# Attention of a two-part transformer block: heads one by one from three bf16 parts, and two heads on row halves from two fp16 parts

## What is computed

```python
    h = _layernorm(x, axis=-1) * (1 + ca) + sa
    x = x + ga * _L0_attn_ref(h, ...)
    h = _layernorm(x, axis=-1) * (1 + cb) + sb
    x = x + gb * _L0_ffn_ref(h, ...)
...
        Q, K, V = proj(Wq, bq), proj(Wk, bk), proj(Wv, bv)     # each (B * H, L, 16)
        _, top_idx = jax.lax.top_k(jnp.linalg.norm(Q, axis=2), 409)
        Q_sel = jnp.take_along_axis(Q, top_idx[:, :, None], axis=1)
        scores = jnp.einsum('bud,bld->bul', Q_sel, K) * scale
        attn = jax.nn.softmax(scores, axis=-1)
        out_full = zeros.at[jnp.arange(BH)[:, None], top_idx].set(jnp.einsum('bul,bld->bud', attn, V))
```

## Time and profile before

| what | value |
|---|---|
| three runs | 1193.07, 1194.58, 1196.31 us; median 1194.58 |
| profiled execution, its span from first to last instruction | 1193.6 us |
| profiled execution's own time | not printed apart from its span; the median lies 1.0 us above the span |
| project block, last product of TensorE to the first of the next block | 121.9 to 134.6 us |
| attend block, first DVE instruction to last | 221.9 to 623.7 us |
| TensorE busy / DVE / ACT / POOL over the span | 83% / 76% / 54% / 60% |
| mean granted TensorE clock | 0.908 of full speed |

### The profile page before, as it was taken

One profiled execution on the slowest core, in us unless ns is written; L12 is line 12 of the kernel. 1 busy time (PEld: TensorE's weight loads), 2 busy tenths in 40 slices (PEclk: granted clock), 3 DMA queues, 4 the chain that ended last, 5 costly groups with the idle time before them and its releaser, 6 DMA issues. The chain is left out here.

```text
span 1193.6 us, 29414 instructions
## 1 busy us (share of the span) xinstructions
PE 993.4 (83%) x7725; PEld 611.1 (51%) x7726; DVE 904.4 (76%) x2197; ACT 646.3 (54%) x1448; POOL 713.0 (60%) x840
## 2 busy tenths in 40 slices
PE   7999101399999999999977873299999999999995
PEld 4444000233333333333324662287778888888894
DVE  4895588778888888888866887667778777777774
ACT  2777185157777777777763441355454444444441
POOL 1687482447888888888659992124445544554443
PEclk9999655569999999999997895599999999999998
DMA  6244772201111111111306991399982322322332
GB/s 229 105 143 164 234 243 79 59 19 44 39 47 34 46 34 46 34 46 34 84 21 205 259 272 41 77 235 226 218 204 50 50 43 48 53 44 44 53 45 27
DMA packets 129229, 118.70 MB, mean 99 GB/s; under 512 B 18128, under 2 KB 117136, under 8 KB 129168
## 3 DMA queue, kind: packets, MB, share of 16 engines
q1 hardware_dynamic: 106904, 95.02, 27.0%
q0 software_dynamic: 20480, 21.53, 11.1%
q10 hardware_dynamic: 1784, 1.44, 0.4%
HBM read 57.27 MB, written 37.60 MB: 79 GB/s over the span
## 5 line engine op out<-in xcount | busy, mean ns | idle before, releaser
L994 DVE TENSOR_REDUCE attend_mxh<-attend_p_a 128x1 f32<-128x512 f32 x416 | 264.1, 685 | 56.9 <-PE attend_p_a L1137 52.0
L1076 ACT ACTIVATE w<-attend_p_b 128x409 f32<-128x409 f32 x480 | 228.8, 514 | 95.1 <-PE attend_p_b L1153 89.3
L1875 ACT ACTIVATE expert_hr<-expert_p,b1t 128x256 f32<-128x256 f32 (+1 forms) x376 | 134.3, 423 | 194.1 <-PE expert_p L1813 174.1
L1768 POOL DMA_INDIRECT out_x<-expert_ys,expert_drop x72 | 121.2, 1684 | 193.6 <-DVE expert_ys L1910 138.2
L1153 PE MATMUL attend_p_b<-attend_qt,w 98*128 98x409 bf16 x480 | 164.4, 347 | 0.3 <-ACT w L1076 0.3
L1137 PE MATMUL attend_p_a<-w,attend_qt 96*128 96x512 bf16 x384 | 151.0, 397 | 1.8 <-DVE attend_mxh L994 0.9
L1835 PE MATMUL expert_p<-w,expert_hhi 128*128 x800 | 136.7, 273 | 0.5 <-DVE expert_ys L1910 0.2
L1813 PE MATMUL expert_p<-expert_xhi,w 128*128 128x256 f16 x800 | 136.3, 273 | 0.0
L1758 POOL DMA_INDIRECT expert_xs<-h_d,expert_take x72 | 73.0, 1014 | 75.4 <-DVE expert_take L1914 54.4
L906 POOL DMA_INDIRECT attend_qsel<-q_d,idx x96 | 92.9, 967 | 39.8 <-POOL attend_idle L934 19.4
L1163 PE MATMUL attend_p_o<-w,attend_vh 128*32 128x409 f32 x1024 | 115.2, 522 | 1.1 <-ACT w L1076 0.6
(11 more groups left out here) (355 smaller groups left out, 1984.4 us busy)
## 6 DMA issues: line engine op xcount, KB each, us to landing
expert_wu<-w SPq DMA_DIRECT2D x88, 256.0 KB
w<-in_L_ffn_w SPq DMA_DIRECT2D x20, 512.0 KB, 4.5
q_d<-project_q SPq DMA_DIRECT2D x32, 256.0 KB, 3.1
w<-k_d SPq DMA_DIRECT2D x32, 192.0 KB
k_d<-project_k SPq DMA_DIRECT2D x45, 128.0 KB
x<-in_L_attn_x SPq DMA_DIRECT2D x8, 512.0 KB
attn_d<-zero SPq DMA_DIRECT2D x8, 512.0 KB
w<-k_d SPq DMA_DIRECT2D x32, 128.0 KB
```

The lines of the kernel that those rows point to most:

```text
L994: dve.tensor_reduce(mxh[:, c, k:k + 1], chunk_bank(a)[:, :], AX, ALU.max).then_inc(a_done, 1)
L1076: act.activation(prob[:, j, :], tile_bank(j)[:, 0:TOP], ACT.Exp, scale=SCALE).then_inc(prob_done, 1)
L1768: pool.indirect_dma_start(out=out, out_offset=bass.IndirectOffsetOnAxis(ap=drop[u][:, s:s + 1], axis=0), in_=ys[u][:, s, :], in_offset=Non ...
L1875: last = act.activation(hr[g % 2][:, f, rows], p_1[g][:, f, rows], ACT.Relu, bias=cst["b1t"][:, bass.ds(e[s] * FB + 2 * g + f, 1)], scale= ...
```

## The change

Q and K are split into two fp16 parts instead of three bf16 parts; the projected Q and K carry a factor UNIT = 16 that the exponential's scale takes out again. A query row in q3_d keeps its 64 numbers: first part twice, zeros, second part. K has two parts in k3_d. In attend two heads form a pair p, one on rows 0 to 63 of kt and of the turned queries (qa, qb), one on rows 64 to 127: 32 rows of K's two parts, 16 rows of a constant 256, 16 rows of the first part again. Each chunk and tile is then two products, with 64 rows each, at array rows 0 and 64 and into two banks. There are four banks p_a for chunks and turned queries and three p_b for tiles and the queries with their maxima. The maxima, divided by 256 and in two parts, are added by products into the rows of the constant (turn_m). The queries are turned twice, for the chunks (turn_q) and for the tiles with the maxima (turn_m). The loop over the 16 pairs is written out. POOL's turn has a scratch row of 256 elements everywhere. The last pair's seven scatters are done in route.

```diff
-TERMS = 6
-PARTS = 3
+PARTS = 2
 HELD = 4
-STACK_K = ((0, 3), (3, 2), (5, 1))
-KR = TERMS * HD
+ROWS_H = HELD * HD
+UNIT = 16.0
+STEP_M = 256.0
...
-                def third(t):
-                    pool.wait_ge(part1_done, t + 1)
-                    pool.tensor_tensor(q3[t % 8][:, :, 3, :], heads(rest[t % R]), q3[t % 8][:, :, 2, :], ALU.subtract).then_inc(part2_done, 1)
...
+                    pool.tensor_tensor(q3[t % 8][:, :, 3, :], heads(y[t % R]), q3[t % 8][:, :, 1, :], ALU.subtract).then_inc(part1_done, 1)
...
-                    dve.tensor_scalar(yk[1][:, :], p_k[1][:, :], bkb[:, 1, B - 1:B], None, ALU.add).then_inc(last_y[1], 1)
...
                     for oc in range(KD):
-                        dve.wait_ge(last_y[oc], 1)
                         dve.wait_ge(last_first[oc], 1)
-                        dve.tensor_tensor(krest[oc][:, :], yk[oc][:, :], k3[(NB - 1) % 2][oc][:, 0, :], ALU.subtract).then_inc(last_rest, 1)
...
+                        dve.scalar_tensor_tensor(out=k3[j % 2][oc][:, 1, :], in0=p_k[oc][:, :], scalar=bkb[:, oc, B - 1:B], in1=k3[j % 2][oc][:, 0, :],
+                                                 op0=ALU.add, op1=ALU.subtract).then_inc(last_second, 1)
...
+                def load_rows(p, h):
+                    sp.dma_start(kt[p % KB][HP * h:HP * h + 32, :], io["k3_d"][2 * p + h].rearrange("r d l -> (r d) l")).then_inc(k_here[p % KB], 16)
+                def load_again(p, h):
+                    sp.dma_start(kt[p % KB][HP * h + 48:HP * h + 64, :], io["k3_d"][2 * p + h, 0]).then_inc(k_here[p % KB], 16)
...
+                def turn(p, at):
+                    pool.memset(idle[:, :], 0.0).then_inc(idled, 1)
+                    pool.wait_ge(idled, next(rows))
+                    wait(pool, a_done, min(CHP * (p + 1) + 6 + 2 * at, CHP * NP))
...
+                def spread_v(p):
+                    wait(pool, pv_ps, BLOCKS * (p - 1))
+                    pool.tensor_copy(vh[p % 2][:, :, :, 0:HD], vn[:, :, 2 * p:2 * p + 2, :]).then_inc(vh_done, 1)
...
+                for p in range(KB):
+                    for h in range(2):
+                        dve.memset(kt[p][HP * h + 32:HP * h + 64, :], STEP_M).then_inc(fill_done, 1)
...
+                for p in range(NP):
+                    maxima(p + 1, 3)
+                    if p > 0:
+                        finish(p - 1)
+                    for a in range(4, NA):
+                        maxima(p + 1, a)
+                    if p + 1 < NP:
+                        minus_maximum(p + 1)
+                    for a in range(3):
+                        maxima(p + 2, a)
...
+                    for h in range(2):
+                        use = tile_use(p, j, h)
+                        wait_tile_bank(pe, use)
+                        rows = slice(HP * h, HP * h + HP)
+                        pe.matmul(p_b[use % 3][:, 0:TOP], kt[p % KB][rows, j * P:(j + 1) * P], qb[p % 2][rows, 0:TOP],
+                                  start=True, stop=True, tile_position=(HP * h, 0)).then_inc(b_ps, 1)
...
+                    scores_tile(p, 14)
+                    scores_chunk(p + 2, 0)
+                    turn_m(p + 1)
+                    scores_chunk(p + 2, 1)
+                    scores_tile(p, 15)
+                    values(p, 6)
+                    scores_chunk(p + 2, 2)
...
-        scattered = sem("scattered")
+        scattered, LAST = sem("scattered"), 2 * (QT - 1) + 1
...
-                    if isinstance(t, int) and t < QT:
+                    if isinstance(t, int) and t < LAST:
                         scatter_last(t)
```

More of the change, by code:

```diff
@@ L1097, in _ @@
-                steps(act, run)
-                products(N - 1)
+                        for h in range(2):
+                            probability(p, j, h)
+                        if j == 0 and p > 0:
+                            products(p - 1)
+                        if j == 7 and p + 2 < NP:
+                            queries(p + 2)
+                        if j == 14 and p + 1 < NP:
+                            queries_max(p + 1)
+                products(NP - 1)
             @block.tensor
@@ L1156, in values @@
[L1156 to L1164 removed]
+                        pe.wait_ge(q_done, q + 1)
@@ L1226, in _ @@
-                steps(pe, run)
-                values(N - 1, U - 1, GRP - 1)
-                results(N - 1, U - 1)
+                turn_q(0)
+                for a in range(TURN_AT):
+                    scores_chunk(0, a)
+                turn_q(1)
+                for a in range(TURN_AT, NA):
+                    scores_chunk(0, a)
+                scores_chunk(1, 0)
+                turn_m(0)
+                scores_chunk(1, 1)
+                scores_chunk(1, 2)
+                pe.wait_ge(fold_done, 1)
```

674 lines of the change are left out of this document (331 added, 343 removed).

## The result

The changed kernel takes 1148.26 us (median of 4 runs, 1147.57 to 1153.04) against 1193.82 of before (4 runs): a ratio of 0.963, 95% interval 0.961 to 0.965. The profiled execution took 1148.46 with a span of 1146.7, against 1193.6. Predicted was 1151, faster. On which chip the changed kernel ran is not known.

A forecast was written before the change was run, and what follows sets the result against it. TensorE was taken to set the pace before, 23.3 us for two heads. Attend -40.0, project -1.5 and -5.4, route +3.4 sum to -43.5, from a median of 1194.6 to 1151 us; range 1132 to 1192.

The forecast's parts named there:

- TensorE's halves overlap: Attend loop: products on the two row halves run side by side, TensorE needing 16.5 us a pair, 21.9 without overlap.
- DVE 17.8 plus waits of 1.6: Attend loop: DVE's work and waits become longer than TensorE's and set a period of 19.4 us a pair.
- POOL 21.55 a pair: Attend loop: POOL falls behind, its slack of 12.3 is used up, and pairs 6 to 12 cost 14.4 us in all.
- Start of the block: Attend's start: eight fills by DVE at 1.76 instead of four, putting the first max rows (M) at 255.3.
- a first M later than 255: Attend's start: one sign set for the prediction being wrong, the first max rows (M) coming after 255 us.
- Loop: Attend's pairs after the first M: 2 for pair 0 at 1.2 GHz, 15 x 19.4, and 14.4 for POOL.
- Project and its end: Project block: Q and K's third part goes, -1.5 us, and fewer steps and stores at its end, -5.4.
- Select: Select block: its instructions are the same in length, so a change of 0.
- Rival 1: Attend loop: POOL holds nothing up, its lag absorbed or its turns shorter; 1137 us, chance 0.13.
- Rival 2: Attend loop: the row halves don't overlap, a period of 22.5 to 23.2; 1192 us (1186 to 1200), chance 0.13.
- Rival 3: Attend loop: TensorE's order stalls it more, since a tile pair shares three banks; period 22, 1175 us, chance 0.07.
- Rival 4: Attend loop: TensorE's clock falls; gain gone at 41% of its work slow, 1217 us at half; chance 0.07.

The follow-up runs named there:

- fills_act: Changed kernel with ACT instead of DVE filling K's constant rows in two of the four places; 1139.26 us, ratio 0.954.
- no_scratch: Changed kernel with POOL's turn lacking its scratch row and the wait for it; 1129.95 us on one chip, 1205.82 when repeated on another.
- two_sources: Changed kernel with the three copies and the multiplication of DVE's minus-maximum step made two-operand operations; 1146.63 us, ratio 0.960.
- turn512: Changed kernel with POOL's scratch row at 512 elements again instead of 256; 1181.22 us, ratio 0.988.
- same_rows: Changed kernel with both products of every chunk, tail chunk and tile pair on array rows 0 to 63; 1191.26 us fastest, others 1217.34 to 1229.43.
- ns_finish: no_scratch with DVE finishing a pair one chunk pair later, after the maxima of chunk 4 instead of 3; 1164.75 us, ratio 0.977.

## Why the prediction was right, step by step

The time (1148 for 1151) and the mechanisms were right. The terms stand less well than the sum: the start is 3.3 longer than worked out and the loop 8.2 shorter, so that the sum lies within 3 us is in part luck.

- **TensorE's halves overlap, 16.5 a pair.** Right, shown from both sides: 0.19 and 0.21 a pair on two row halves, 0.35 and 0.44 on one. TensorE's room was as forecast, and only because of it could another engine become the bound. The rule of the Trainium skill ("TensorE: Matmul & The Clock Gate", Part 3), that products on different row groups run at once, holds here.
- **DVE 17.8 plus waits of 1.6, a period of 19.4.** The work was right: 26 maxima in a row take 15.63 in fills_act, and 1.24 and 0.89 stand above. The waits were too high: no_scratch and two_sources run at 18.9, so they are 1.1 (0.56 ahead of the finish, 0.20 in two places, the rest in small pieces). The other 0.5 of the 19.4 measured was a cost that I had not in the sum, DVE's one-operand operations held up by POOL. The period was right for a reason half wrong, by luck.
- **POOL 21.55 a pair, slack 12.3, holding the spread of V; 14.4.** The mechanism and its place were right, and turn512 confirms the slope. The pace is 21.0, so the lag grows by 1.6 instead of 2.15, and the first wait came in pair 9 rather than about 6. It costs 7.3 of waits and the slow clock behind the two longest; the six last periods are 20.75 on average, not 21.5, and exceed 19.4 by 8.1 together. The prediction took the hold-ups without any effect on the clock.
- **Start of the block, first M at 255.3 on the old clock, 32.8 from the block's first fill.** It is 36.1. I multiplied the fill's 1.76 by eight and passed over the "[0.48 <-issue]" that stands in that very row. Seven more times 0.48 is 3.4, the whole miss. On the old clock the first M is at 258.6, so the sign that the prediction set for being wrong, a first M later than 255, came; it was set 0.3 under the prediction's own 255.3, and what failed was this term alone.
- **Loop.** 2 + 15 x 19.4 + 14.4 = 307.4; 299.2 measured. The 2 for pair 0 at the low clock was too much: the first period is 19.95. **Last pair** 21; 22.5. Together with the start the block is 357.7 against 361.2, each from the first fill; before it was 401.2 so counted, which makes -43.5 instead of -40.0 (the -44.1 above counts from the first instruction of before, a short one ahead of the fills).
- **Project and its end, -6.9.** TensorE's last products for K end 1.4 earlier (116.93 + 3.60 for 118.33 + 3.60); predicted 1.5. With two stores of 1.01 each, not 1.36, select starts 8.0 earlier (126.80 for 134.76).
- **Select, 0.** It lost 1.8 with its barrier: attend's first DVE instruction is only 6.2 earlier. One operation has 1.04 of it, 1.79 long where it took 0.75 before, and it stands beside an operation of POOL's that had ended before it began in the kernel before (188.05 for 189.80):

```profile
182.15 1.79 DVE L729 SCALAR_TENSOR_TENSOR select_nv<-select_cum,select_room,select_hit 128x512 f32<-128x512 f32 x1
```

```profile
180.65 2.74 POOL L651 TENSOR_TENSOR w<-w 128x1024 f16<-128x1024 f32 x1 [0.25 <-ACT w L659]
```

  So "the same in length" was wrong: the instructions are the same, but in the changed kernel this one meets another on POOL. In all the variants' traces it takes 1.79 or more as well.
- **Route, +3.4.** The rest behind attend is longer by 3.4. **Around the span** the prediction kept 1.0; in the changed kernel's profiled execution it is 1.8.
- **The rivals.** Rival 1 (POOL holds nothing, 1137) is not what happened but was nearly on the mark for the price: take POOL's pace and its interference away and the kernel takes 1130. Rival 2 would have been 1192; same_rows' fastest run is 1191, with a stretch of low clock of unknown length in it, so that this is so near is partly chance. Rival 3 is out: no period of the first ten is over 20.2. Rival 4, the clock, shows after pair 0 in two windows of 8 us and nowhere else in the loop, so at a few per cent, not 41. In fills_act it shows in five such windows between 424 and 496, and in ns_finish the eight pairs with it are 17.5 us longer than with 20.0 each, of the 32.4 lost in the loop.

What the runs correct most is POOL's part: I had it as one wait, and it is three things, its pace, the clock behind the longer waits, and DVE's small operations. Of the 18 us between the changed kernel and no_scratch they are the 15.9 of the loop: 4.6 in the first nine periods, where nobody waits for POOL (174.7 less nine at 18.9), and 11.1 in the last six (124.5 less six at 18.9; the 0.2 that is missing is rounding of the 18.9).

## What to carry to other kernels

When one engine's own time falls, work out the pace of each of the others for a whole loop and its slack, as here: the next bound is then a number, and where it appears can be named before the run. Read the bracket behind the operation that is multiplied: a start-to-start distance is the price, a duration is not. And try a gain that comes from removing a pause on more than one chip, with its runs next to the kernel before, ahead of believing it: no_scratch was 0.945 on one and 1.006 on another. And an operation beside another engine's can be longer than alone: where a change moves blocks against each other, expect a microsecond here and there that no instruction count shows.

## What the hardware showed that was not expected

- **DVE's one-operand operations on SBUF wait for POOL.** A copy of 0.16 took up to 1.51, a multiplication of 0.18 up to 1.27. A clear case: DVE's copy ends at 309.69, 0.02 after POOL's memset.

```profile
309.31 0.38 DVE L1006 COPY attend_mxh<-attend_mxh 25x2 f32<-25x2 f32 x1
```

```profile
309.34 0.33 POOL L912 MEMSET attend_idle<- 128x256 f32 x1
```

  Reductions and operations with two operands kept 0.15 to 0.20 beside memsets. The Trainium skill ("SBUF — State Buffer", Who interferes with whom) says the same: copy and tensor_scalar can take a port that DVE shares with GpSimd, an exclusive lock for the whole instruction, tensor_reduce never does, and two SBUF inputs meet GpSimd only where it reads. The trace agrees in all three, the last by the 0.39 and 0.60 of two_sources beside POOL's copy and by the 1.79 in select. It is not the whole: of the twenty operations of the step that took 0.28 or more in the changed kernel, eight overlap a memset or a copy of POOL's (4.1 us above their usual time), but twelve lie inside the record of a transfer alone (2.2 us), while in no_scratch such operations beside a transfer kept 0.16 to 0.23. What holds those twelve is open.
- **A memset costs more than its record.** 1.76 is shown, 2.24 from one to the next. By "VectorE: DVE Perf Modes" of the Trainium skill (Zero memsets can be issued as uint32) a memset takes one cycle per element whatever the type, which for these 2048 would be an estimated 2.13 at that page's 0.96 GHz; the trace agrees with the distance rather than the duration. The page puts zeros in as 32-bit words to save half of that; whether it does so for this constant was not tried.
- **The clock can fall behind a short wait, and the length of the wait alone does not tell.** At half clock a value product takes 0.89 instead of 0.53 and a group of eight 1.59 instead of 0.89. The waits of 2.27 to 4.56 for the spread (thirteen, in the changed kernel, turn512, two_sources and fills_act) all had such products behind them. Of the shorter ones 1.40 in the changed kernel had none, but 0.93 and 0.98 in two_sources and 0.66 in fills_act had, and the 1.35 and 1.46 of ns_finish had them in eight pairs and not in six.
- **The clock can stay low under work.** In the profiled execution of same_rows TensorE was busy 96.00 of 96.00 us from 264 to 360 at 0.50, before 1.00 was granted; the kernel before, busy without a gap from 264 to 320 too, had 1.00 there.
- **Without pauses between POOL's transfers other engines stood still on two of four chips**, up to 3.5 us at a time in the loop, until POOL paused, and the kernel took 76 us more (1206 for 1130). What they waited for is open.
